# Householder steps of a small eigensolver: divisor from root times size plus square sum, reflector written by VectorE, square sum first on TensorE

## The chip, the core and the metric

The kernel runs on one core of a Trainium2 chip. A core has TensorE (matmuls), VectorE and ScalarE (elementwise work), GpSimd, and DMA queues; each engine runs its own list of instructions in order, and the engines wait for one another by semaphores. The metric is the device time of one execution in microseconds (us), the median of three runs. For this kernel a difference below 0.2% can't be told from none.

## The reference

A two-layer network over x of shape (128, 64, 128), with a normalized adjacency matrix of 64x64. Cut to what matters here:

```python
def _L0_gnn_ref(features, A, W1, b1, W2, b2):
    deg = jnp.sum(A, axis=0) + jnp.sum(A, axis=1) - jnp.diagonal(A)
    d_inv_sqrt = jnp.where(deg > 0, jax.lax.rsqrt(deg), 0.0)
    L = jnp.diag(deg) - A
    L_norm = d_inv_sqrt[:, None] * L * d_inv_sqrt[None, :]
    _, U = jnp.linalg.eigh(L_norm)
    agg = jnp.einsum('mn,bnd->bmd', U.T, features)
    h = jax.nn.relu(agg @ W1 + b1)
    out = h @ W2 + b2
    return jnp.einsum('nm,bmd->bnd', U, out)

x = x + _L0_gnn_ref(_layernorm(x), adj, ...)     # needs all eigenvectors of a 64x64 matrix
x = x + _L0_ffn_ref(_layernorm(x), ...)          # 8 experts, 2 per token
x = x + _L1_gnn_ref(_layernorm(x), adj, ...)     # aggregation, two batch norms
x = x + _L1_ffn_ref(_layernorm(x), ...)          # a shared and 8 routed experts
```

## The kernel before

The program is written by hand, engine by engine: what stands in `tridiagonal_vector` is VectorE's list, `tridiagonal_tensor` TensorE's, `tridiagonal_scalar` ScalarE's. No scheduler moves anything. Before the first layer can start, the eigenvectors of the 64x64 matrix must be there, and everything else of the kernel comes after them. The eigensolver has these stages: preparation (to 13 us), 62 Householder steps that make the matrix tridiagonal (to 193 us), sections that find the eigenvalues, eigenvectors of the tridiagonal matrix, the basis change, and three refinements. The layers follow.

A step k works on the trailing matrix A with t = 63 - k rows and takes the column t as its vector. It has three lists:

- TensorE (L171 to L191) makes six products from the column, broadcast over all partitions: in `ps[0]` its last element alpha, in `ps[1]` its square sum, in `ps[2]` the column's products with A, in `ps[5]` and `ps[3]` rows of A broadcast, in `ps[4]` a product that is only read after the steps. Each counts one up in `hh_pe` (NP = 6 a step).
- VectorE (L133 to L168) makes the sign of alpha (L149), G = sign x root (L151), G(alpha+G) (L152), a guard against zero (L153), the reciprocal (L154), then T = row x G + products (L157), B = T x y - A (L160), a sum over B x VR (L163) and the new A (L167). It counts in `hh_dve` (ND = 9).
- ScalarE (L194 to L222) takes the root (L205), copies the products (L207), writes the reflector v into `VV` (L209), copies the first part of VR (L212), writes y = v x reciprocal into `YY` (L215), VR's tail (L216) and VRT (L218). It counts in `hh_act` (NA = 7). Besides, in the last 54 steps it makes two sums each for the first layer norm (`first_norm_sum`: L1007, L1017), which nothing in the steps needs. A sum is an activation and a read of its accumulator.

The next step's products start when A is written (L183). SBUF tiles of the eigensolver are all named `u` in the profile, PSUM banks `bank`. All tiles of a step begin at partition 0.

Of the kernel before, what the change touches and what calls it, by code (L numbers as in the profile page):

```python
# [8 lines left out]
ALU = mybir.AluOpType  # L9
# [3 lines left out]
N = 64  # L13
P = 128
D = 128
STEPS = N - 2
# [6 lines left out]
ND, NP, NA = 9, 6, 7  # L23
# [109 lines left out]
def tridiagonal_vector(nc, dve, S, E, m, ps):  # L133
# [4 lines left out]
    alpha, row = ps[0][0:N, 0:1], ps[5]  # L138
    for k in range(STEPS):
        t, j = at_step(k)  # L140
        b = k * ND

        def step(n, ins, wait=True):
            ins.then_inc(hd, 1)
            if wait:
                dve.wait_ge(hd, b + n)
        G = SS[:, k:k + 1]
        dve.wait_ge(hp, k * NP + 1)
        step(1, V.tensor_scalar(c[:, 0:1], alpha, 0.0, 2.0, ALU.is_ge, ALU.mult))  # L149
        dve.wait_ge(ha, k * NA + 1)  # L150
        step(2, V.scalar_tensor_tensor(out=G, in0=c[:, 0:1], scalar=-1.0, in1=c[:, 7:8], op0=ALU.add, op1=ALU.mult))  # L151
        step(3, V.scalar_tensor_tensor(out=c[:, 1:2], in0=alpha, scalar=G, in1=G, op0=ALU.add, op1=ALU.mult))  # L152
        step(4, V.tensor_scalar(c[:, 2:3], c[:, 1:2], 1e-36, None, ALU.max))  # L153
        step(5, V.reciprocal(c[:, 6:7], c[:, 2:3]), False)  # L154
        dve.wait_ge(hp, k * NP + 4)
        dve.wait_ge(ha, k * NA + 2)
        step(6, V.scalar_tensor_tensor(out=m["T"][0:t, 0:t], in0=row[0:t, 0:t], scalar=SS[0:t, k:k + 1],  # L157
                                       in1=m["QA"][0:t, 0:t], op0=ALU.mult, op1=ALU.add))
        dve.wait_ge(ha, k * NA + 5)
        step(7, V.scalar_tensor_tensor(out=m["B"][0:t, 0:t], in0=m["T"][0:t, 0:t], scalar=m["YY"][0:t, k:k + 1],  # L160
                                       in1=A[0:t, 0:t], op0=ALU.mult, op1=ALU.subtract))
        dve.wait_ge(ha, k * NA + 6)
        step(8, V.scalar_tensor_tensor(out=m["hjunk"][0:t, 0:t], in0=m["B"][0:t, 0:t], scalar=1.0, in1=m["VR"][0:t, 0:t],  # L163
                                       op0=ALU.mult, op1=ALU.mult, accum_out=c[0:t, 5:6]))
        dve.wait_ge(ha, k * NA + 7)
        dve.wait_ge(hp, k * NP + 6)
        step(9, V.scalar_tensor_tensor(out=A[0:t, 0:t], in0=m["VRT"][0:t, 0:t], scalar=c[0:t, 5:6], in1=m["B"][0:t, 0:t],  # L167
                                       op0=ALU.mult, op1=ALU.subtract))  # L168


def tridiagonal_tensor(nc, pe, S, E, C, m, ps):  # L171
# [5 lines left out]
    for k in range(STEPS):  # L177
# [8 lines left out]
        from_column(ps[0][0:N, 0:1], t, t, unit[0:t, j:j + 1])  # L186
        from_column(ps[1][0:N, 0:1], t, t, A[0:t, t:t + 1])
        from_column(ps[2][0:N, 0:t], t, t, A[0:t, 0:t])
# [5 lines left out]
def tridiagonal_scalar(nc, act, S, E, C, m, ps, t):  # L194
# [3 lines left out]
    A, VR, SS, c = m["AI"][:, N:2 * N], m["VR"], m["SS"], m["c"]  # L198
    unit = C[0:N, C_ID:C_ID + N]
    sums = 0  # L200
    for k in range(STEPS):
        n, j = at_step(k)
        b = k * ND
        act.wait_ge(hp, k * NP + 2)
        F.activation(c[:, 7:8], ps[1][0:N, 0:1], ACT.Sqrt).then_inc(ha, 1)  # L205
        act.wait_ge(hp, k * NP + 3)
        F.copy(m["QA"][0:n, 0:n], ps[2][0:n, 0:n]).then_inc(ha, 1)  # L207
        act.wait_ge(hd, b + 2)
        F.activation(m["VV"][0:n, k:k + 1], unit[0:n, j:j + 1], ACT.Identity, scale=SS[0:n, k:k + 1],  # L209
                     bias=A[0:n, n:n + 1]).then_inc(ha, 1)  # L210
# [3 lines left out]
        act.wait_ge(ha, k * NA + 3)  # L214
        F.activation(m["YY"][0:n, k:k + 1], m["VV"][0:n, k:k + 1], ACT.Copy, scale=c[0:n, 6:7]).then_inc(ha, 1)  # L215
        F.activation(VR[0:n, j:n], ps[3][0:n, j:n], ACT.Identity, bias=SS[0:n, k:k + 1]).then_inc(ha, 1)  # L216
        act.wait_ge(ha, k * NA + 6)
        F.activation(m["VRT"][0:n, 0:n], VR[0:n, 0:n], ACT.Copy, scale=c[0:n, 6:7]).then_inc(ha, 1)  # L218
        if k >= STEPS - EARLY_SUMS // 2:
            first_norm_sum(nc, act, S, E, t, sums)  # L220
            first_norm_sum(nc, act, S, E, t, sums + 1)
            sums += 2  # L222
# [1738 lines left out]
```

## Time and profile before

| | us |
|---|---|
| median of 3 runs | 1445.71 (1445.41 to 1447.09) |
| the profiled execution | 1447.26 |
| its span, first to last instruction | 1445.5 |
| busy over the span: matmul / VectorE / ScalarE / GpSimd | 1094.5 / 934.2 / 650.7 / 605.5 |
| mean granted TensorE clock | 0.936 of full speed |

In the rows below, PE is TensorE's matmuls, PEld its weight loads, DVE VectorE, ACT ScalarE. A group such as `u<-bank 64x1` writes tile u from a PSUM bank, 64 partitions by 1 element. The shares over the whole span say little, since the stages differ: the steps at the head of the kernel are a chain of short instructions on three engines, and the experts at its end keep TensorE full. The page's list of the chain that ended last reaches back only to 1229 us; for the steps one reads the timeline of a single step and the waits.

### The profile page before, as it was taken

How to read it: one execution, taken by the hardware profiler on the slowest of the kernel's cores; microseconds unless marked ns; L12 is line 12 of the kernel's file. 1: busy time of each engine (PE TensorE's matmuls, PEld its weight loads, DVE VectorE, ACT ScalarE, POOL GpSimd, SP SyncE). 2: the span in 40 equal slices, each digit the busy share in tenths (PEclk: the TensorE clock that was granted, in tenths of full speed). 3: DMA queues.
4: the chain of work that ended last, by engine and by line, in shares of the span. 5: the costliest groups of instructions: out<-in, count | busy, mean ns of one | idle time of the engine just before them, and what ended most of it. 6: DMA issues, size and time to landing. Idle time of an engine off the chain costs nothing. (4 is left out here: it accounts for less than half of the span.)

```text
span 1445.5 us, 23166 instructions
## 1 busy us (share of the span) xinstructions
PE 1094.5 (76%) x6172; PEld 887.7 (61%) x6172; DVE 934.2 (65%) x3416; ACT 650.7 (45%) x1813; POOL 605.5 (42%) x591
## 2 busy tenths in 40 slices
PE   3454577514877299999999587779998898899990
PEld 3444465413655288888888443355554797799990
DVE  5555578875788656656667585886743555465673
ACT  3777765600444122222222288547764344344440
POOL 3000000000154777777764530023344677777754
PEclk9999999999998599999999889869999899899995
DMA  9993000000010132222234340000001222222436
GB/s 224 428 428 168 1 2 0 1 0 0 9 38 30 52 81 79 69 87 81 76 110 123 115 159 1 0 14 22 25 30 45 76 87 73 87 84 82 146 104 232
DMA packets 59265, 125.45 MB, mean 87 GB/s; under 512 B 13132, under 2 KB 39636, under 8 KB 57600
## 3 DMA queue, kind: packets, MB, share of 16 engines
q0 software_dynamic: 20000, 73.21, 13.5%
q1 hardware_dynamic: 39136, 50.78, 13.0%
q8 instruction: 50, 0.82, 0.3%
q14 instruction: 79, 0.65, 0.2%
HBM read 50.77 MB, written 74.99 MB: 87 GB/s over the span
## 5 line engine op out<-in xcount | busy, mean ns | idle before, releaser
L891 POOL DMA_INDIRECT rows<-pay,slot x256 | 261.6, 1022 | 483.4 <-issue 432.1
L1224 POOL DMA_INDIRECT planes<-work,goal x284 | 300.1, 1057 | 130.7 <-issue 57.7
L1371 PE MATMUL bank<-pay 128*128 128x128 f32 (+1 forms) x1988 | 276.1, 280 | 0.0
L1371 PEld LDWEIGHTS bank<-pay 128*128 128x128 f32 (+1 forms) x1988 | 263.6, 193 | 10.6 <-DVE pay L1304 0.4
L1331 ACT ACTIVATE pay<-bank,pay 128x256 f32<-128x256 f32 x284 | 125.8, 474 | 167.8 <-PE bank L1362 167.8
L1327 ACT ACTIVATE pay<-bank 128x256 f32<-128x256 f32 (+1 forms) x213 | 81.4, 382 | 246.6 <-PE bank L1360 212.1
L1362 PE MATMUL bank<-pay 128*128 128x256 f32 x568 | 136.9, 385 | 2.2 <-DVE pay L1266 2.2
L1359 PE MATMUL bank<-pay 128*128 128x256 f32 (+1 forms) x426 | 128.9, 384 | 0.6 <-DVE pay L1266 0.6
L181 PE MATMUL bank<-consts,u 63*64 63x1 f32 (+61 forms) x372 | 60.4, 274 | 89.7 <-DVE u L167 88.9
L1360 PE MATMUL bank<-pay 128*128 128x256 f32 (+1 forms) x426 | 128.4, 383 | 0.0
L1304 DVE TENSOR_TENSOR pay<-pay,bank 128x256 f32<-128x256 f32 (+1 forms) x213 | 88.9, 417 | 59.5 <-PE bank L1371 30.7
L1256 DVE COPY pay<-wreg 128x1066 f32 (+1 forms) x142 | 103.6, 730 | 26.8 <-issue 26.8
L1362 PEld LDWEIGHTS bank<-pay 128*128 128x128 f32 x568 | 104.2, 194 | 14.1 <-DVE pay L1256 2.5
L181 PEld LDWEIGHTS bank<-consts,u 63*64 63x64 f32 (+61 forms) x372 | 51.3, 215 | 95.1 <-DVE u L167 94.1
L1360 PEld LDWEIGHTS bank<-pay 128*128 128x128 f32 (+1 forms) x426 | 76.8, 180 | 16.9 <-issue 0.3
L1359 PEld LDWEIGHTS bank<-pay 128*128 128x128 f32 (+1 forms) x426 | 71.5, 181 | 11.2 <-issue 1.1
L1347 PE MATMUL bank<-consts,pay 128*128 128x128 f32 x284 | 55.6, 278 | 27.5 <-DMA pay<-rows 27.5
L1562 PE MATMUL bank<-work,wreg 128*128 128x512 f32 x128 | 65.3, 612 | 5.8 <-ACT work L1617 5.6
L1266 DVE COPY pay<-bank 128x256 f32<-128x256 f32 x142 | 59.4, 418 | 15.3 <-PE bank L1347 15.2
L1278 DVE TENSOR_TENSOR pay<-bank,pay 128x256 f32<-128x256 f32 x71 | 30.1, 424 | 57.9 <-PE bank L1371 57.7
L1555 PE MATMUL bank<-work,wreg 128*128 128x512 f32 x128 | 63.4, 598 | 0.0
L366 PE MATMUL bank<-u,consts 128*128 128x28 f32 (+1 forms) x192 | 54.5, 395 | 7.7 <-DVE u L301 5.6
(399 smaller groups left out, 1988.1 us busy)
## 6 DMA issues: line engine op xcount, KB each, us to landing
rows<-pay POOLq DMA_DIRECT2D x10, 3432.0 KB, 55.7
pay<-rows SPq DMA_DIRECT2D x142, 130.0 KB, 2.2
u<-planes SPq DMA_DIRECT2D x64, 256.0 KB, 3.4
planes<-work,goal POOLq DMA_INDIRECT x284
wreg<-in_w SPq DMA_DIRECT2D x1, 4264.0 KB, 24.8
wreg<-in_w SPq DMA_DIRECT2D x1, 4112.0 KB, 13.4
X<-in_x SPq DMA_DIRECT2D x2, 2048.0 KB, 20.2
rows<-pay,slot POOLq DMA_INDIRECT x256, 2.3
```

Of the source, the lines that this page charges most:

```text
L181: T.matmul(out, A[0:rows, col:col + 1].to_broadcast([rows, N]), rhs, start=True, stop=True).then_inc(hp, 1)
L891: return self.nc.gpsimd.indirect_dma_start(out=xs, out_offset=bass.IndirectOffsetOnAxis(ap=self.t["slot"][:, k, q:q + 1], axis=0), in_=sel ...
L1224: nc.gpsimd.indirect_dma_start(out=planes, out_offset=bass.IndirectOffsetOnAxis(ap=t["goal"][:, j * 2 + h:j * 2 + h + 1], axis=0), in_=t[" ...
L1256: V.tensor_copy(t["wst"][j % 2][:, 0:WB[layer]], W[:, bass.ds(expert * WB[layer], WB[layer])]).then_inc(s("w"), 1)
L1304: V.tensor_tensor(t["hh"][c][0:w, :], t["hs"][c][0:w, :], ps[c][0:w, TS:2 * TS], ALU.mult).then_inc(s("hh"), 1)
L1327: A.activation(t["hs"][c][0:w, :], ps[c][0:w, 0:TS], ACT.Silu).then_inc(s("hs"), 1)
L1331: A.activation(t["hh"][c], ps[c][:, 0:TS], ACT.Gelu, bias=t["wst"][j % 2][:, 2 * CH1 * P + c:2 * CH1 * P + c + 1]).then_inc(s("hh"), 1)
L1359: T.matmul(ps[c][0:n, 0:TS], w[:, a:a + n], x, start=True, stop=True)
L1360: T.matmul(ps[c][0:n, TS:2 * TS], w[:, HID0 + a:HID0 + a + n], x, start=True, stop=True).then_inc(s("up"), 1)
L1362: T.matmul(ps[c][:, 0:TS], w[:, c * P:(c + 1) * P], x, start=True, stop=True).then_inc(s("up"), 1)
L1371: ins = T.matmul(ps[4 + j % 2][:, h * P:(h + 1) * P], t["hh"][c][0:n, h * P:(h + 1) * P], t["wst"][j % 2][0:n, at + c * P:at + (c + 1) * P ...
L1562: T.matmul(ps[4][:, :], t["WS"][:, (CH1 + c) * P:(CH1 + c + 1) * P], t["sh"][c % 2], start=(c == 0), stop=(c == CH1 - 1)).then_inc(S("a1_d ...
```

## The change

- TensorE: the square sum (`ps[1]`) is now the first product, and the second writes two columns of `ps[0]`: alpha and the square sum once more. For this a strided operand takes column j of the identity and column t of A in one product, so the left half of `AI` has to hold the identity; it is copied there once, ahead of the steps.
- VectorE: the divisor is no longer made as G(alpha+G) but as beta = root x size + square sum, with size = sign x alpha, and the guard acts on the square sum. VectorE now writes the reflector v and y itself. 12 instructions a step for 9.
- ScalarE: v and y are gone, 5 counted instructions for 7. VR's tail waits for G, VRT for the reciprocal. One of the two normalization sums moves from the step's end to between the root and the copy of the products.
- The matmuls behind the steps that read `VV` and `YY` wait for VectorE instead of ScalarE.

```diff
 PASSES = len(POINTS)
 REFINE = 3
 BIG = 1e15
-ND, NP, NA = 9, 6, 7
+ND, NP, NA = 12, 6, 5
 LEVELS = 6
 EARLY_SUMS = 108
 SCALE_AT = 9
@@ -130,42 +130,53 @@
     return trailing, trailing - 1
 
 
-def tridiagonal_vector(nc, dve, S, E, m, ps):
+def tridiagonal_vector(nc, dve, S, E, C, m, ps):
 
     V, c, SS = nc.vector, m["c"], m["SS"]
     hd, hp, ha = S("hh_dve"), S("hh_pe"), S("hh_act")
     A = m["AI"][:, N:2 * N]
-    alpha, row = ps[0][0:N, 0:1], ps[5]
+    unit = C[0:N, C_ID:C_ID + N]
+    alpha, square, row = ps[0][0:N, 0:1], ps[0][0:N, 1:2], ps[5]
+    sign, size, guarded, beta, inverse, root = (c[:, i:i + 1] for i in (0, 1, 2, 3, 6, 7))
     for k in range(STEPS):
         t, j = at_step(k)
-        b = k * ND
-
-        def step(n, ins, wait=True):
-            ins.then_inc(hd, 1)
-            if wait:
-                dve.wait_ge(hd, b + n)
-        G = SS[:, k:k + 1]
-        dve.wait_ge(hp, k * NP + 1)
-        step(1, V.tensor_scalar(c[:, 0:1], alpha, 0.0, 2.0, ALU.is_ge, ALU.mult))
+        G, v, y = SS[:, k:k + 1], m["VV"][0:t, k:k + 1], m["YY"][0:t, k:k + 1]
+
+        def done(n):
+            dve.wait_ge(hd, k * ND + n)
+        dve.wait_ge(hp, k * NP + 2)
+        V.tensor_scalar(sign, alpha, 0.0, 2.0, ALU.is_ge, ALU.mult).then_inc(hd, 1)
+        V.tensor_scalar(guarded, square, 1e-36, None, ALU.max).then_inc(hd, 1)
+        done(1)
+        V.scalar_tensor_tensor(out=size, in0=sign, scalar=-1.0, in1=alpha, op0=ALU.add, op1=ALU.mult).then_inc(hd, 1)
+        done(3)
         dve.wait_ge(ha, k * NA + 1)
-        step(2, V.scalar_tensor_tensor(out=G, in0=c[:, 0:1], scalar=-1.0, in1=c[:, 7:8], op0=ALU.add, op1=ALU.mult))
-        step(3, V.scalar_tensor_tensor(out=c[:, 1:2], in0=alpha, scalar=G, in1=G, op0=ALU.add, op1=ALU.mult))
-        step(4, V.tensor_scalar(c[:, 2:3], c[:, 1:2], 1e-36, None, ALU.max))
-        step(5, V.reciprocal(c[:, 6:7], c[:, 2:3]), False)
+        V.scalar_tensor_tensor(out=beta, in0=root, scalar=size, in1=guarded, op0=ALU.mult, op1=ALU.add).then_inc(hd, 1)
+        V.scalar_tensor_tensor(out=G, in0=sign, scalar=-1.0, in1=root, op0=ALU.add, op1=ALU.mult).then_inc(hd, 1)
+        done(4)
+        V.reciprocal(inverse, beta).then_inc(hd, 1)
+        done(5)
+        V.scalar_tensor_tensor(out=v, in0=unit[0:t, j:j + 1], scalar=SS[0:t, k:k + 1], in1=A[0:t, t:t + 1], op0=ALU.mult,
+                               op1=ALU.add).then_inc(hd, 1)
         dve.wait_ge(hp, k * NP + 4)
         dve.wait_ge(ha, k * NA + 2)
-        step(6, V.scalar_tensor_tensor(out=m["T"][0:t, 0:t], in0=row[0:t, 0:t], scalar=SS[0:t, k:k + 1],
-                                       in1=m["QA"][0:t, 0:t], op0=ALU.mult, op1=ALU.add))
+        V.scalar_tensor_tensor(out=m["T"][0:t, 0:t], in0=row[0:t, 0:t], scalar=SS[0:t, k:k + 1],
+                               in1=m["QA"][0:t, 0:t], op0=ALU.mult, op1=ALU.add).then_inc(hd, 1)
+        done(7)
+        V.tensor_tensor(y, v, inverse[0:t, :], ALU.mult).then_inc(hd, 1)
+        done(9)
+        V.scalar_tensor_tensor(out=m["B"][0:t, 0:t], in0=m["T"][0:t, 0:t], scalar=y,
+                               in1=A[0:t, 0:t], op0=ALU.mult, op1=ALU.subtract).then_inc(hd, 1)
+        done(10)
+        dve.wait_ge(ha, k * NA + 4)
+        V.scalar_tensor_tensor(out=m["hjunk"][0:t, 0:t], in0=m["B"][0:t, 0:t], scalar=1.0, in1=m["VR"][0:t, 0:t],
+                               op0=ALU.mult, op1=ALU.mult, accum_out=c[0:t, 5:6]).then_inc(hd, 1)
+        done(11)
         dve.wait_ge(ha, k * NA + 5)
-        step(7, V.scalar_tensor_tensor(out=m["B"][0:t, 0:t], in0=m["T"][0:t, 0:t], scalar=m["YY"][0:t, k:k + 1],
-                                       in1=A[0:t, 0:t], op0=ALU.mult, op1=ALU.subtract))
-        dve.wait_ge(ha, k * NA + 6)
-        step(8, V.scalar_tensor_tensor(out=m["hjunk"][0:t, 0:t], in0=m["B"][0:t, 0:t], scalar=1.0, in1=m["VR"][0:t, 0:t],
-                                       op0=ALU.mult, op1=ALU.mult, accum_out=c[0:t, 5:6]))
-        dve.wait_ge(ha, k * NA + 7)
         dve.wait_ge(hp, k * NP + 6)
-        step(9, V.scalar_tensor_tensor(out=A[0:t, 0:t], in0=m["VRT"][0:t, 0:t], scalar=c[0:t, 5:6], in1=m["B"][0:t, 0:t],
-                                       op0=ALU.mult, op1=ALU.subtract))
+        V.scalar_tensor_tensor(out=A[0:t, 0:t], in0=m["VRT"][0:t, 0:t], scalar=c[0:t, 5:6], in1=m["B"][0:t, 0:t],
+                               op0=ALU.mult, op1=ALU.subtract).then_inc(hd, 1)
+        done(12)
 
 
 def tridiagonal_tensor(nc, pe, S, E, C, m, ps):
@@ -183,8 +194,8 @@
             pe.wait_ge(hd, k * ND)
         else:
             pe.wait_ge(*E.at("lap_flipped"))
-        from_column(ps[0][0:N, 0:1], t, t, unit[0:t, j:j + 1])
         from_column(ps[1][0:N, 0:1], t, t, A[0:t, t:t + 1])
+        from_column(ps[0][0:N, 0:2], t, t, m["AI"][0:t, j:j + N + 2:N + 1])
         from_column(ps[2][0:N, 0:t], t, t, A[0:t, 0:t])
         from_column(ps[5][0:N, 0:t], t, j, unit[0:t, 0:t])
         from_column(ps[3][0:N, 0:t], t, t, unit[0:t, 0:t])
@@ -195,31 +206,28 @@
 
     F = nc.scalar
     hd, hp, ha = S("hh_dve"), S("hh_pe"), S("hh_act")
-    A, VR, SS, c = m["AI"][:, N:2 * N], m["VR"], m["SS"], m["c"]
-    unit = C[0:N, C_ID:C_ID + N]
+    VR, SS, c = m["VR"], m["SS"], m["c"]
     sums = 0
     for k in range(STEPS):
         n, j = at_step(k)
         b = k * ND
-        act.wait_ge(hp, k * NP + 2)
+        act.wait_ge(hp, k * NP + 1)
         F.activation(c[:, 7:8], ps[1][0:N, 0:1], ACT.Sqrt).then_inc(ha, 1)
+        if k >= STEPS - EARLY_SUMS // 2:
+            first_norm_sum(nc, act, S, E, t, sums)
+            sums += 1
         act.wait_ge(hp, k * NP + 3)
         F.copy(m["QA"][0:n, 0:n], ps[2][0:n, 0:n]).then_inc(ha, 1)
-        act.wait_ge(hd, b + 2)
-        F.activation(m["VV"][0:n, k:k + 1], unit[0:n, j:j + 1], ACT.Identity, scale=SS[0:n, k:k + 1],
-                     bias=A[0:n, n:n + 1]).then_inc(ha, 1)
         act.wait_ge(hp, k * NP + 5)
         F.copy(VR[0:n, 0:j], ps[3][0:n, 0:j]).then_inc(ha, 1)
         act.wait_ge(hd, b + 5)
-        act.wait_ge(ha, k * NA + 3)
-        F.activation(m["YY"][0:n, k:k + 1], m["VV"][0:n, k:k + 1], ACT.Copy, scale=c[0:n, 6:7]).then_inc(ha, 1)
         F.activation(VR[0:n, j:n], ps[3][0:n, j:n], ACT.Identity, bias=SS[0:n, k:k + 1]).then_inc(ha, 1)
-        act.wait_ge(ha, k * NA + 6)
+        act.wait_ge(hd, b + 6)
+        act.wait_ge(ha, k * NA + 4)
         F.activation(m["VRT"][0:n, 0:n], VR[0:n, 0:n], ACT.Copy, scale=c[0:n, 6:7]).then_inc(ha, 1)
         if k >= STEPS - EARLY_SUMS // 2:
             first_norm_sum(nc, act, S, E, t, sums)
-            first_norm_sum(nc, act, S, E, t, sums + 1)
-            sums += 2
+            sums += 1
 
 
 def basis_tensor(nc, pe, S, E, C, m, ps):
@@ -227,7 +235,7 @@
 
     T = nc.tensor
     ident, flip = C[0:N, C_ID:C_ID + N], C[0:N, C_FLIP:C_FLIP + N]
-    pe.wait_ge(S("hh_act"), STEPS * NA)
+    pe.wait_ge(S("hh_dve"), STEPS * ND)
     T.matmul(ps[7][0:N, 0:N], m["VV"], m["YY"], start=True, stop=True).then_inc(*E.on("qb_gram"))
     T.matmul(ps[5][0:N, 0:N], m["VV"], flip, start=True, stop=True)
     T.matmul(ps[5][0:N, N:2 * N], m["YY"], flip, start=True, stop=True).then_inc(S("qb_turned"), 1)
@@ -428,11 +436,12 @@
     ch(V.memset(AHB[:, :], 0.0))
     for h in (0, N):
         ch(V.tensor_tensor(AHB[h:h + N, h:h + N], m["Ah"][h:h + N, :], ps[0][h:h + N, N:2 * N], ALU.mult))
+    ch(V.tensor_copy(m["AI"][:, 0:N], ident))
     dve.wait_ge(*E.at("lap_whole"))
     V.tensor_copy(m["AI"][:, N:2 * N], ps[1][0:N, 0:N]).then_inc(*E.on("lap_flipped"))
     dve.wait_ge(*E.at("lap_flipped"))
 
-    tridiagonal_vector(nc, dve, S, E, m, ps)
+    tridiagonal_vector(nc, dve, S, E, C, m, ps)
 
     SS, AI, F = m["SS"], m["AI"], m["F"]
     dve.wait_ge(S("hh_dve"), STEPS * ND)
```

VectorE's list for the first step (63 rows), before. `u1` holds the eigensolver's tiles, `bank0` alpha, `bank5` the broadcast row:

```order
L149 TENSOR_SCALAR u1<-bank0 64x1
L151 SCALAR_TENSOR_TENSOR u1<-u1 64x1
L152 SCALAR_TENSOR_TENSOR u1<-bank0,u1 64x1
L153 TENSOR_SCALAR u1<-u1 64x1
L154 RECIPROCAL u1<-u1 64x1
L157 SCALAR_TENSOR_TENSOR u1<-bank5,u1 63x63
L160 SCALAR_TENSOR_TENSOR u1<-u1 63x63
L163 SCALAR_TENSOR_TENSOR u1<-u1 63x63
L167 SCALAR_TENSOR_TENSOR u1<-u1 63x63
```

The same step after the change:

```order
L441 COPY u1<-bank1 64x64
L148 TENSOR_SCALAR u1<-bank0 64x1
L149 TENSOR_SCALAR u1<-bank0 64x1
L151 SCALAR_TENSOR_TENSOR u1<-u1,bank0 64x1
L154 SCALAR_TENSOR_TENSOR u1<-u1 64x1
L155 SCALAR_TENSOR_TENSOR u1<-u1 64x1
L157 RECIPROCAL u1<-u1 64x1
L159 SCALAR_TENSOR_TENSOR u1<-consts,u1 63x1
L163 SCALAR_TENSOR_TENSOR u1<-bank5,u1 63x63
L166 TENSOR_TENSOR u1<-u1 63x1
L168 SCALAR_TENSOR_TENSOR u1<-u1 63x63
L172 SCALAR_TENSOR_TENSOR u1<-u1 63x63
```

Sign and guard (L148, L149) now stand together, beta (L154) ahead of G (L155), v (L159) ahead of T (L163), and y (L166) between T and B (L168).

ScalarE's list for the step with 52 rows, one with two normalization sums (L1007 before, L1016 after), before:

```order
L205 ACTIVATE u1<-bank1 64x1
L207 COPY u1<-bank2 52x52
L209 ACTIVATE u1<-consts,u1 52x1
L212 COPY u1<-bank3 52x51
L215 ACTIVATE u1<-u1 52x1
L216 ACTIVATE u1<-bank3,u1 52x1
L218 ACTIVATE u1<-u1 52x52
L1007 ACTIVATE u1<-X 128x128 x2
```

The same step after the change:

```order
L215 ACTIVATE u1<-bank1 64x1
L1016 ACTIVATE u1<-X 128x128
L220 COPY u1<-bank2 52x52
L222 COPY u1<-bank3 52x51
L224 ACTIVATE u1<-bank3,u1 52x1
L227 ACTIVATE u1<-u1 52x52
L1016 ACTIVATE u1<-X 128x128
```

v (L209) and y (L215 before) are gone, and the first sum stands behind the root (L215 after).

## Rows read from the trace of the kernel before

**Rows 1.** Busy time by stretch: the steps, then the rest of the eigensolver

```profile
core 0: us, PE busy (x) PEld busy (x) DVE busy (x) ACT busy (x) POOL busy (x), PEclk, DMA share, GB/s
13.40:192.90 179.50, 89.17 (x744) 83.84 (x744) 102.52 (x621) 130.80 (x648) 5.80 (x12) 1.00 0.63 240
192.90:371.00 178.10, 97.94 (x403) 78.74 (x404) 131.65 (x562) 62.76 (x240) 0.00 (x0) 0.99 0.00 1
```

**Rows 2.** Waits from 13 to 193 us: total, times, longest

```profile
DVE u L160 <- ACT u L215: 16.4, 62, 0.3
DVE u L151 <- ACT u L205: 16.4, 62, 0.3
```

**Rows 3.** Timeline of the step with 47 rows: start, duration, instruction, [idle before]

```profile
60.90 0.37 PE L181 MATMUL bank<-consts,u 47*64 47x1 f32 x2 [1.50 <-DVE u L167]
...
61.13 0.64 PE L181 MATMUL bank<-u 47*64 47x1 f32 x4
61.38 0.15 DVE L149 TENSOR_SCALAR u<-bank 64x1 f32<-64x1 f32 x1 [0.54 <-PE bank L181]
...
61.52 0.16 ACT L205 ACTIVATE u<-bank 64x1 f32<-64x1 f32 x1 [0.48 <-PE bank L181]
...
61.79 0.15 DVE L151 SCALAR_TENSOR_TENSOR u<-u 64x1 f32<-64x1 f32 x1 [0.26 <-ACT u L205]
61.80 0.19 ACT L207 COPY u<-bank 47x47 f32<-47x47 f32 x1
...
61.98 0.21 DVE L152 SCALAR_TENSOR_TENSOR u<-bank,u 64x1 f32<-64x1 f32 x1
...
62.22 0.14 DVE L153 TENSOR_SCALAR u<-u 64x1 f32<-64x1 f32 x1
...
62.40 0.15 DVE L154 RECIPROCAL u<-u 64x1 f32<-64x1 f32 x1
62.48 0.26 DVE L157 SCALAR_TENSOR_TENSOR u<-bank,u 47x47 f32<-47x47 f32 x1
62.59 0.29 ACT L215 ACTIVATE u<-u 47x1 f32<-47x1 f32 x1
62.79 0.24 ACT L216 ACTIVATE u<-bank,u 47x1 f32<-47x1 f32 x1
62.99 0.26 DVE L160 SCALAR_TENSOR_TENSOR u<-u 47x47 f32<-47x47 f32 x1 [0.25 <-ACT u L215]
63.06 0.33 ACT L218 ACTIVATE u<-u 47x47 f32<-47x47 f32 x1
63.28 0.20 DVE L163 SCALAR_TENSOR_TENSOR u<-u 47x47 f32<-47x47 f32 x1
...
63.52 0.26 DVE L167 SCALAR_TENSOR_TENSOR u<-u 47x47 f32<-47x47 f32 x1
...
63.84 0.37 PE L181 MATMUL bank<-consts,u 46*64 46x1 f32 x2 [1.50 <-DVE u L167]
```

**Rows 4.** Timeline: VectorE instructions that don't wait for their predecessor

```profile
5.87 0.15 DVE L397 TENSOR_SCALAR u<-u 64x1 f32<-64x1 f32 x1
5.94 0.14 DVE L398 TENSOR_SCALAR u<-u 64x1 f32<-64x1 f32 x1
...
197.03 0.22 DVE L455 TENSOR_SCALAR u<-bank 64x62 f32<-64x62 f32 x1
197.16 0.14 DVE L456 COPY u<-bank 64x1 f32<-64x1 f32 x1
```

**Rows 5.** All instructions of L157: duration in ns, shortest, median, longest

```profile
L157 DVE SCALAR_TENSOR_TENSOR u<-bank,u x62: 207/241/275, 15.0 to 191.6; 63x63 f32<-63x63 f32 x1, 62x62 f32<-62x62 f32 x1, 61x61 f32<-61x61 f32 x1, 60x60 f32<-60x60 f32 x1
```

**Rows 6.** Timeline of ScalarE: two normalization sums in a late step

```profile
189.58 0.38 ACT L1017 ACTIVATE u<-X,u 128x128 f32<-128x128 f32 x1
...
189.97 0.38 ACT L1017 ACTIVATE u<-X,u 128x128 f32<-128x128 f32 x1
```

**Rows 7.** Timeline of VectorE just ahead of the first step

```profile
12.62 0.47 DVE L430 TENSOR_TENSOR AHB<-u,bank 64x64 f32<-64x64 f32 x2
13.13 0.22 DVE L432 COPY u<-bank 64x64 f32<-64x64 f32 x1
```

## The prediction

> **What bounds the kernel now.** I read first the busy time by stretch. From 13.40 to 192.90 us the kernel does only the 62 Householder steps: 179.5 us with TensorE's matmuls busy for 89, VectorE for 103 and ScalarE for 131 [rows 1]. No engine is full, so this stretch is a chain of waits. 179.5/62 is 2.90 us a step. The stretch behind it, to 371 us, has no DMA traffic to speak of (1 GB/s) and VectorE busy for 132 of 178 us [rows 1]: the rest of the eigensolver is a VectorE chain that starts from the last step. What a step loses or gains therefore moves everything behind it.
>
> Next, who waits for whom in that stretch. Besides the waits at the step's start for TensorE, VectorE waits twice for ScalarE in every step: 62 times at L151 for the square root and 62 times at L160 for y from L215, 16.4 us each, so 0.26 us a time [rows 2].
>
> Then one step in order of time, that with 47 rows (it starts at 60.90, the next at 63.84: 2.94 us) [rows 3]. I count from its first matmul (t = 0). VectorE reads alpha's sign at 0.48 (L149), ScalarE takes the root at 0.62 (L205), and the chain runs L151 0.89, L152 1.08, L153 1.32, L154 1.50, L215 on ScalarE 1.69, L160 2.09, L163 2.38, L167 2.62, next matmul 2.94. T (L157, 1.58) and the work of L207, L216 and L218 lie beside it. Each of these starts is the end of the one before plus a handover, which the rows give: 0.04 within VectorE (61.79+0.15 to 61.98), 0.04 VectorE to ScalarE (62.55 to 62.59), 0.11 ScalarE to VectorE (62.88 to 62.99), 0.06 VectorE to TensorE.
>
> **What an instruction costs if nothing waits for it.** The change puts three VectorE instructions more into a step (12 for 9) and three ScalarE instructions less of its own chain (5 for 7, and one normalization sum moved), so it matters how long an instruction keeps the engine's queue. Rows show it: L154 starts at 62.40 and lasts 0.15, yet L157 starts at 62.48 [rows 3]; L397 to L398 is 0.07 at 0.15 of duration; L455, which reads a bank, gives way after 0.13 of 0.22 [rows 4]. So a successor that does not wait starts about 0.08 before the duration ends; a dependent one 0.04 after. I use both.
>
> **The new step, part by part** (t from its first matmul).
> The matmul order: the square sum is now first, alpha and the square sum together second. The spacing of two products is 0.23 (60.90 to 61.13) [rows 3]. The root's input comes one product earlier, so the root starts at 0.62-0.22 = 0.40 and is there for VectorE at 0.40+0.16+0.11 = 0.67. VectorE's first instruction waits for the second product: 0.48+0.22 = 0.70, a loss of 0.22 at the start that the removed wait of 0.26 about pays for.
> Sign 0.70; "guarded" in its shadow at 0.77. Size needs the sign: 0.70+0.15+0.04 = 0.89. It has a constant scalar, as L151 (0.15); with a pointer scalar the form takes 0.21 (L152) [rows 3]. Beta (root times size plus guarded, pointer scalar) 0.89+0.19 = 1.08; the root is ready since 0.67, so ScalarE leaves this part of the chain. G may follow beta after 0.21-0.08 = 0.13: 1.21. The reciprocal needs beta: 1.33. The reflector v needs G: 1.21+0.19 = 1.40, which is also when the reciprocal gives way. v has a pointer scalar (0.21) and ends at 1.61. T takes its shadow at 1.53 and keeps the queue for its duration less 0.08; it lasts 0.207 to 0.275, median 0.241 [rows 5], so until 1.66 to 1.73, 1.69 at the median. y needs v (1.65) and the queue: 1.69. It lasts 0.15, and B starts at 1.69+0.19 = 1.88 (1.85 to 1.92).
> Before, B (L160) started at 2.09 [rows 3]. Behind B nothing changes: the same three instructions with the same handovers. Gain 0.21 a step; I take off 0.01 for beta, which now has a second, already satisfied wait (L167 with three waits comes 0.02 later behind its predecessor than the others), and get 0.20. 62 x 0.20 = 12.4 us.
>
> What must stay hidden. T needs the copy of the products, at 0.90 (L207), done at 1.09 and visible at 1.20, against T at 1.53. The tail of VR needs G: 1.36+0.04 = 1.40. Ahead of it in ScalarE's queue stands the copy of VR's first part, whose product is two spacings (0.43) behind that which L207 waits for: 1.33, so the tail starts at some 1.43 and ends at 1.67, 1.78 for VectorE, against the junk product at 1.88+0.29 = 2.17. VRT follows the tail by 0.27 and lasts 0.33: 2.03, visible at 2.14, against the last instruction at 1.88+0.53 = 2.41. Slack 0.27; if it went, each excess would count 62 times. The sum now between root and product copy, in 54 of the steps, keeps ScalarE for 0.39 in its longer form (189.58 to 189.97) [rows 6]: from 0.48 to 0.87, before the copy's 0.90. The sum that remains at the end runs into the next step's idle time of ScalarE.
> One copy of the identity (64x64) is added ahead of the steps, before L432, which does not wait for TensorE in the trace (it stands right behind L430) [rows 7]. So it is on the path, once: about L432's own 0.22 us.
> The final wait for the reflectors costs nothing: the last of them are now written before the last A.
>
> **Sum.** 12.4-0.2 = 12.2 us off. The profiled execution took 1447.26 us with a span of 1445.5; it becomes 1435.1, its span 1433.3. The median of the runs, 1445.71, lies 1.55 below that execution, so the forecast is 1445.71-12.2 = 1433.5 us.
>
> **Where the Trainium skill says otherwise.** The bank read at L149 lasts 0.151 us, the same kind of instruction on SBUF 0.15 (L397) [rows 3, 4]. The Trainium skill, page "VectorE: DVE Perf Modes", section on the TRN2 errata, has a fixed 120 cycles for a PSUM source against 58 for SBUF at 0.96 GHz, an estimate of 0.065 us more. By that rule "size", which reads alpha from a bank, would add 0.065 to each step and the sum would be 8.2 us; by the trace it adds nothing.
>
> **Rivals.**
> (a) The queue costs less than I reckon, or the second product reaches VectorE earlier. If T did not delay y (B at 1.84) and the sign started at 0.66 instead of 0.70, half way to ScalarE's 0.62: gain 0.29, 18.0-0.2 = 17.8 us, 1427.9. For it: ScalarE sees the second product at 0.62. Against: VectorE's own 0.48 for the first product is a steady row.
> (b) The queue costs more: T, reading a bank and SBUF with a pointer, holds y for its whole duration (y at 1.53+0.24+0.04 = 1.81, B at 2.00), or a bank read that lasts 0.21 delays size by 0.06, or both. Gain 0.03 to 0.15; at 0.09 it is 5.6-0.2 = 5.4 us, 1440.3. No row has a short instruction right behind one of T's form, so this is open.
> (c) The other sign: VectorE does not overlap in this mix, each instruction starts only when its predecessor has ended. Place: the nine instructions from sign to y. Price: 0.151+0.151+0.151+0.21+0.151+0.155+0.21+0.241+0.15 = 1.57 and nine handovers of 0.03 (a dependent pair takes 0.04): B at 0.70+1.57+0.27 = 2.54, 0.45 later than now, +28 us, 1474. It decides from the point where the added queue time exceeds 0.20 a step. Against: the shadow of L154 over L157 in this very loop. The Trainium skill, same page, section "The DRAIN you can't avoid", says that after every operation the next one does not start until the pipe is empty; that would be this case. The trace speaks against it in rows 3 and 4.
> (d) No gain to see: ScalarE becomes late behind its own queue (VRT past 2.41 by some 0.2 or more), or a stretch of lower TensorE clock behind the eigensolver falls differently and takes the gain. Result 1443 to 1448. Against: 0.27 of slack, and the clock was 1.00 and 0.99 in the two stretches up to 371 us [rows 1].
> (e) The change does not do what it says: VectorE still waits for the root or for ScalarE's y. The first has 0.41 of slack (0.67 against 1.08), the second no longer exists. I give it nothing of its own.
>
> **Chances.** Forecast 0.64 (its own range 1430 to 1437), (a) 0.10, (b) 0.18, (d) 0.04, (c) 0.04. The range for 8 in 10 takes the forecast and the nearer part of (a) and (b): 1428 to 1440. A difference of over 0.2% (2.9 us) can be told from none for this kernel; (b) lies below 1442.8 in nearly all of its span. Faster 0.92, the same 0.04, slower 0.04.
>
> **What the profile after would show.** A step of about 2.74 us at 47 rows and a stretch of steps of about 167 us; no wait of VectorE for ScalarE at all; sign at 0.70, beta at 1.08, v at 1.40, B at 1.88 behind the first matmul; the root at 0.40 and the product copy still at 0.90 behind a sum. Wrong would be: y more than 0.2 behind T (b), G more than 0.2 behind beta (c), a wait of VectorE for ScalarE at the junk product or the last instruction (d). The stretches behind the steps should keep their lengths; if one does not, the sum is wrong though each step is right.

## The result, and the profile after

| | before | after |
|---|---|---|
| median of 4 runs each, us | 1446.33 | 1432.59 |
| ratio, 95% interval | | 0.9907 (0.9895 to 0.9919) |
| span of the profiled execution, us | 1445.5 | 1430.5 |
| the 62 steps, first matmul to the diagonal's read | 179.5 | 166.0 |

The change gained 13.7 us; 12.2 were forecast (1433.5 us), and 1432.6 lies in the range. The two spans differ by more, 15.0, because the profiled execution before (1447.26 us) was longer than its kernel's median. Busy time by stretch, the steps and the rest of the eigensolver, as [rows 1]:

```profile
core 0: us, PE busy (x) PEld busy (x) DVE busy (x) ACT busy (x) POOL busy (x), PEclk, DMA share, GB/s
13.60:179.60 166.00, 89.17 (x744) 83.82 (x744) 109.46 (x806) 96.08 (x525) 5.80 (x12) 1.00 0.68 260
179.60:357.70 178.10, 97.12 (x412) 77.95 (x413) 132.31 (x566) 62.90 (x240) 0.00 (x0) 1.00 0.00 1
```

The second stretch has kept its length. VectorE does 7 us more in the steps, ScalarE 35 less. Waits from 13 to 181 us (total, times, longest): those of [rows 2] are gone, and what VectorE still waits for in every step is TensorE at its start.

```profile
PE bank L192 <- DVE u L177: 75.7, 61, 1.6
ACT u L215 <- PE bank L192: 49.8, 62, 6.1
DVE u L148 <- PE bank L192: 46.7, 62, 1.1
```

The step with 47 rows, as [rows 3] (start, duration, instruction):

```profile
58.33 0.87 PE L192 MATMUL bank<-u 47*64 47x1 f32 x6 [1.37 <-DVE u L177]
58.73 0.16 ACT L215 ACTIVATE u<-bank 64x1 f32<-64x1 f32 x1 [0.81 <-PE bank L192]
...
59.02 0.15 DVE L148 TENSOR_SCALAR u<-bank 64x1 f32<-64x1 f32 x1 [0.75 <-PE bank L192]
59.10 0.14 DVE L149 TENSOR_SCALAR u<-bank 64x1 f32<-64x1 f32 x1
59.21 0.15 DVE L151 SCALAR_TENSOR_TENSOR u<-u,bank 64x1 f32<-64x1 f32 x1
...
59.39 0.21 DVE L154 SCALAR_TENSOR_TENSOR u<-u 64x1 f32<-64x1 f32 x1
...
59.52 0.14 DVE L155 SCALAR_TENSOR_TENSOR u<-u 64x1 f32<-64x1 f32 x1
59.63 0.15 DVE L157 RECIPROCAL u<-u 64x1 f32<-64x1 f32 x1
...
59.71 0.20 DVE L159 SCALAR_TENSOR_TENSOR u<-consts,u 47x1 f32<-47x1 f32 x1
...
59.84 0.25 DVE L163 SCALAR_TENSOR_TENSOR u<-bank,u 47x47 f32<-47x47 f32 x1
60.02 0.14 DVE L166 TENSOR_TENSOR u<-u 47x1 f32<-47x1 f32 x1
...
60.19 0.26 DVE L168 SCALAR_TENSOR_TENSOR u<-u 47x47 f32<-47x47 f32 x1
...
61.04 0.87 PE L192 MATMUL bank<-u 46*64 46x1 f32 x6 [1.28 <-DVE u L177]
```

Counted from the step's first matmul: sign 0.69 (forecast 0.70), size 0.88 (0.89), beta 1.06 (1.08), G 1.19 (1.21), v 1.38 (1.40), T 1.51 (1.53), y 1.69 (1.69), B 1.86 (1.88), next step 2.71 (2.74). The copy of the identity takes 0.22 ahead of the steps (13.10 to 13.32), as reckoned.

### The profile page after: what moved, and what is told of

Read it like the earlier page. It is cut to its first block and busy times, and to the rows that moved or that the text cites. A ratio compares the mean times of both kernels' runs of the same rounds, so it can differ in the third digit from the quotient of the medians.

```text
span 1430.5 us, 23168 instructions
## 1 busy us (share of the span) xinstructions
PE 1092.2 (76%) x6172; PEld 885.5 (62%) x6172; DVE 941.3 (66%) x3603; ACT 615.7 (43%) x1689; POOL 605.2 (42%) x591
## 5 line engine op out<-in xcount | busy, mean ns | idle before, releaser
L1380 PEld LDWEIGHTS bank<-pay 128*128 128x128 f32 (+1 forms) x1988 | 263.4, 193 | 10.7 <-DVE pay L1313 0.7
L192 PE MATMUL bank<-u 63*64 63x1 f32 (+61 forms) x496 | 73.7, 255 | 76.8 <-DVE u L177 75.7
L192 PEld LDWEIGHTS bank<-u 63*64 63x64 f32 (+61 forms) x496 | 64.4, 217 | 82.2 <-DVE u L177 80.9
## 6 DMA issues: line engine op xcount, KB each, us to landing
wreg<-in_w SPq DMA_DIRECT2D x1, 4112.0 KB, 13.3
```

Source lines behind the costliest of these rows:

```text
L192: T.matmul(out, A[0:rows, col:col + 1].to_broadcast([rows, N]), rhs, start=True, stop=True).then_inc(hp, 1)
L1380: ins = T.matmul(ps[4 + j % 2][:, h * P:(h + 1) * P], t["hh"][c][0:n, h * P:(h + 1) * P], t["wst"][j % 2][0:n, at + c * P:at + (c + 1) * P ...
```

## The experiments

Twelve kernels ran. The kernel before took 1445.92 us beside the first four, 1445.53 beside the next four and 1445.56 beside the last four; each ratio goes by its own. "At n rows" is a step; times in a step count from its first matmul.

For small differences the end of the steps is the better measure than the total. Far behind them lies a stretch that no edit touches, from the first layer's last product (L1070 in the changed kernel) to the last mixing product (L1491). In the fourteen profiled executions it took 428.4 to 428.7 us in four and 430.4 to 433.9 in the others, so up to some 3 us of a difference between two kernels need not come from the steps. The steps end where the next stage first reads the diagonal: at 192.9 us before and at 179.6 in the changed kernel.

**Alpha first.** The first two products swapped back:

```diff
-        from_column(ps[1][0:N, 0:1], t, t, A[0:t, t:t + 1])
         from_column(ps[0][0:N, 0:2], t, t, m["AI"][0:t, j:j + N + 2:N + 1])
+        from_column(ps[1][0:N, 0:1], t, t, A[0:t, t:t + 1])
```

(VectorE waits for the first product, ScalarE for the second.)

> The changed kernel with TensorE's first two products swapped back: alpha with the square sum first, the root's square sum second. My theory (starts follow from durations, 0.04 us for a dependent instruction, duration less 0.08 for one that does not wait): sign 0.48, size 0.67, root visible at 0.62+0.27 = 0.89, so beta at 0.89 instead of 1.06 and B some 0.17 earlier; T at 1.34 needs the product copy, which the sum ahead of it delays to about the same time. Step with 47 rows 2.54 us against 2.71, in all 62 x 0.17 = 10.5 us below the changed kernel: 1422. That the square sum comes first would then be the one harmful part of the change. Rival theory: the root is what the chain waits for, and putting the square sum first is part of the gain; then this kernel is slower than the changed one by up to 62 x 0.2 = 12 us, and VectorE waits at beta for ScalarE from 0.9 to 1.1.

Measured 1423.34 us, 0.9840 (0.9824 to 0.9857) of before, 9.3 below the changed kernel; the steps end at 170.1 us, 9.5 earlier. The timeline at 43 rows (its first matmul at 66.30):

```profile
66.78 0.15 DVE L148 TENSOR_SCALAR u<-bank 64x1 f32<-64x1 f32 x1 [0.54 <-PE bank L192]
...
66.92 0.17 ACT L215 ACTIVATE u<-bank 64x1 f32<-64x1 f32 x1 [0.78 <-PE bank L192]
...
67.20 0.21 DVE L154 SCALAR_TENSOR_TENSOR u<-u 64x1 f32<-64x1 f32 x1
...
68.00 0.25 DVE L168 SCALAR_TENSOR_TENSOR u<-u 43x43 f32<-43x43 f32 x1
```

Beta starts at 0.90, B at 1.70, 0.16 earlier. "Square sum first" feeds the root, which had 0.4 us of slack, and holds up alpha, which had none: that part of the change costs 9 us. The rival falls.

**Reflector only.** The old divisor and the old order of products, one product column, no copy of the identity; v and y stay on VectorE (part of the edit against the changed kernel):

```diff
+        V.scalar_tensor_tensor(out=size, in0=alpha, scalar=G, in1=G, op0=ALU.add, op1=ALU.mult).then_inc(hd, 1)
         V.scalar_tensor_tensor(out=v, in0=unit[0:t, j:j + 1], scalar=SS[0:t, k:k + 1], in1=A[0:t, t:t + 1], op0=ALU.mult,
                                op1=ALU.add).then_inc(hd, 1)
+        done(3)
+        V.tensor_scalar(guarded, size, 1e-36, None, ALU.max).then_inc(hd, 1)
+        done(5)
+        V.reciprocal(inverse, guarded).then_inc(hd, 1)
...
```

> One part alone: v and y on VectorE; divisor G(alpha+G) with its guard, and the order of the products, as before the change. Theory: sign 0.48, G 0.89, u 1.08, v behind it at 1.21, guard 1.33, reciprocal 1.51, T 1.59, y 1.75, B 1.93 against 2.09 before: 0.16 a step, 10 us, 1436.4. So most of the gain of the whole change (13.7 us) comes from this part. Rival: the new divisor, which takes one dependent instruction off the chain, brings most of it, and this kernel stays at 1441 to 1446.

Measured 1434.92 us, 0.9923 (0.9906 to 0.9939): 11.0 us less than before, against 13.7 for the whole change. By the steps alone it is less: they end 8.7 us earlier (at 184.2), against 13.3. B at 1.95 (43 rows) to 1.89 (3 rows). Alpha first has the same products' order and the new divisor besides, and its steps end 14.1 us before those of this kernel (11.6 by the medians). So the new divisor is worth much more than this run and the changed kernel suggest, once alpha comes first.

**Reflector on ScalarE.** The other part alone:

```diff
+        act.wait_ge(hd, b + 5)
+        F.activation(m["VV"][0:n, k:k + 1], unit[0:n, j:j + 1], ACT.Identity, scale=SS[0:n, k:k + 1],
+                     bias=A[0:n, n:n + 1]).then_inc(ha, 1)
...
+        F.activation(m["YY"][0:n, k:k + 1], m["VV"][0:n, k:k + 1], ACT.Copy, scale=c[0:n, 6:7]).then_inc(ha, 1)
```

> The other part alone: new divisor, square sum first, but v and y back on ScalarE (10 VectorE instructions, 7 of ScalarE; one normalization sum still behind the root). Theory: G is there only at 1.34 (0.89+0.15 = 1.04 before the change), v on ScalarE at 1.38 lasts 0.39, y at 1.81 lasts 0.29, visible 2.21, so B at 2.21: 0.12 a step later than before and 0.35 later than the changed kernel. 1446.3+7.6 = 1454, slower than both. Rival: y's wait was only 0.26 a step and the shorter divisor pays for it; then 1436 to 1446.

Measured 1456.64 us, 1.0074 (1.0058 to 1.0091), slower than before by 10.7; the steps end 12.0 us later. At 43 rows (first matmul at 76.98):

```profile
78.18 0.14 DVE L155 SCALAR_TENSOR_TENSOR u<-u 64x1 f32<-64x1 f32 x1
...
78.36 0.39 ACT L220 ACTIVATE u<-consts,u 43x1 f32<-43x1 f32 x1 [0.29 <-DVE u L155]
...
78.84 0.29 ACT L226 ACTIVATE u<-u 43x1 f32<-43x1 f32 x1
...
79.24 0.26 DVE L165 SCALAR_TENSOR_TENSOR u<-u 43x43 f32<-43x43 f32 x1 [0.53 <-ACT u L226]
```

G at 1.20 instead of 0.89 sends v and y off late; VectorE now waits 0.53 at B. The two parts do not add up: 11.0 gained by the one, 10.7 lost by the other, 13.7 gained together.

**Sums last.** Both normalization sums at the step's end again (the call between root and product copy moved behind VRT):

```diff
-        if k >= STEPS - EARLY_SUMS // 2:
-            first_norm_sum(nc, act, S, E, t, sums)
-            sums += 1
...
-            sums += 1
+            first_norm_sum(nc, act, S, E, t, sums + 1)
+            sums += 2
```

> The changed kernel with both normalization sums back at the step's end. Theory: they end in ScalarE's idle time (last sum free at 1.72+0.21+0.78 = 2.71, the next root 0.41 behind a step of 2.5 to 2.7), and the one behind the root never delayed the product copy enough to count (T at 1.51, copy visible at 1.15): same time as the changed kernel, 1432.6 within 1.5. Rival: the moved sum is needed for the gain, because two sums at the end push the next root; then up to 54 x 0.1 = 5 us slower.

Measured 1432.11 us, 0.9907 (0.9890 to 0.9923): the move is worth nothing here; the steps end within 0.2 us of the changed kernel's.

**Alpha first, sums last.** Both edits.

> Alpha first as in the run of that name, and both normalization sums back at the step's end. There the product copy started at 1.08 in the late steps behind the longer sum, at 0.84 without it, and T at 1.35 just had it. Theory: T starts at 1.35 by G (1.04), v (1.23) and the queue, not by the copy, so nothing is gained: 1423.3 within 1.5. Rival: T waited for the copy (visible at 1.08+0.15+0.11 = 1.34) and moves to 1.32: 22 steps x 0.03 = 0.7 us, hardly to be told; a gain of over 2 us would mean that ScalarE's queue was on the chain in more places.

Measured 1422.72 us, 0.9833 (0.9812 to 0.9853). T starts at 1.35 as with alpha first alone (43 rows). No gain that can be told.

**G ahead.** The kernel above with VectorE's order changed, and with it the counts that ScalarE waits for:

```diff
+        dve.wait_ge(ha, k * NA + 1)
+        V.scalar_tensor_tensor(out=G, in0=sign, scalar=-1.0, in1=root, op0=ALU.add, op1=ALU.mult).then_inc(hd, 1)
         done(3)
-        dve.wait_ge(ha, k * NA + 1)
         V.scalar_tensor_tensor(out=beta, in0=root, scalar=size, in1=guarded, op0=ALU.mult, op1=ALU.add).then_inc(hd, 1)
-        V.scalar_tensor_tensor(out=G, in0=sign, scalar=-1.0, in1=root, op0=ALU.add, op1=ALU.mult).then_inc(hd, 1)
         done(4)
-        V.reciprocal(inverse, beta).then_inc(hd, 1)
-        done(5)
         V.scalar_tensor_tensor(out=v, ...)
+        done(5)
+        V.reciprocal(inverse, beta).then_inc(hd, 1)
```

> Alpha first, sums last, and on VectorE the order sign, guard, size, G, beta, v, reciprocal, T, y, B: G and v no longer stand behind beta. Theory: the root is visible at 0.89, G 0.90, beta in its shadow 0.98, v 1.11, reciprocal 1.23, T 1.31, y (T's 0.25 less 0.08 behind it) 1.48, B 1.65 at 47 rows, against 1.70 with beta first. 0.05 a step: 3 us below the 1423.3 of alpha first, 1420.3. Rival: the reciprocal, now behind v, sets y (1.23+0.155+0.04 = 1.43, so not) or ScalarE's VRT becomes late (visible 2.10+0.11 against the last instruction at 2.18): then no gain, 1423.

Measured 1416.49 us, 0.9789 (0.9767 to 0.9810), 6.2 below the kernel with both edits where 3 were expected. B starts at 1.57 at 43 rows where 1.65 was expected, since G starts at 0.82 and not at 0.90: 0.04 behind the root's end (0.62+0.16). Before and in the kernel above it was 0.11. There VectorE's instruction behind the root had two waits, here it has one. The timeline at 43 rows (first matmul at 64.89):

```profile
66.46 0.25 DVE L168 SCALAR_TENSOR_TENSOR u<-u 43x43 f32<-43x43 f32 x1
66.66 0.33 ACT L224 ACTIVATE u<-u 43x43 f32<-43x43 f32 x1
...
66.88 0.07 DVE L172 DVE_READ_ACCUMULATOR u<-u 43x1 f32 x1
67.08 0.25 DVE L177 SCALAR_TENSOR_TENSOR u<-u 43x43 f32<-43x43 f32 x1
```

But the 0.08 does not explain the 3 us of surplus. B is 0.13 earlier than in the kernel above, the last instruction (L177) only 0.04: it starts 0.13 behind the accumulator's read where 0.04 was the rule, and 0.09 behind VRT (L224), which has become the limit. The steps end 3.8 us earlier, near the 3 expected; the other 2.4 us lie behind them.

**G ahead, 16 commands.** A command is an entry of VectorE's list: an instruction, a wait that stands in front of one, or the read of an accumulator. A long step takes 0.08 to 0.36 us more than its neighbours. VectorE's wait for its own last instruction goes:

```diff
-        done(12)
```

> The kernel with G ahead, without VectorE's wait for its own last instruction at the end of each step (TensorE waits for it anyway, and VectorE for TensorE). The changed kernel shows steps that are 0.1 to 0.36 us too long every seventh to eighth step, and each time one instruction further on in the step; the kernel before shows none. Theory: VectorE's instructions are fetched in blocks of 128 (8.2 KB, if each wait beyond the first counts as one), and with 18 of them a step the border creeps through the step. This kernel has 16 a step, so long steps come every eighth step and always at the same instruction, or are not to be seen at all. Time within 1.5 us of the kernel with G ahead (its own stalls make some 1.7 us). Rival: the long steps come from memory traffic; then their places do not change with the count.

Measured 1414.72 us, 0.9781 (0.9760 to 0.9802). The timeline at 43 rows (first matmul at 64.58):

```profile
64.99 0.15 DVE L148 TENSOR_SCALAR u<-bank 64x1 f32<-64x1 f32 x1 [0.46 <-PE bank L191]
...
65.20 0.16 ACT L214 ACTIVATE u<-bank 64x1 f32<-64x1 f32 x1 [0.44 <-PE bank L191]
...
65.39 0.15 DVE L153 SCALAR_TENSOR_TENSOR u<-u 64x1 f32<-64x1 f32 x1
...
66.34 0.33 ACT L223 ACTIVATE u<-u 43x43 f32<-43x43 f32 x1
66.44 0.20 DVE L172 SCALAR_TENSOR_TENSOR u<-u 43x43 f32<-43x43 f32 x1
66.56 0.07 DVE L172 DVE_READ_ACCUMULATOR u<-u 43x1 f32 x1
...
66.76 0.25 DVE L177 SCALAR_TENSOR_TENSOR u<-u 43x43 f32<-43x43 f32 x1
```

Sign at 0.41, where it was 0.48 with a second wait; G hangs on the root, so this gives nothing. The steps end 1.0 us earlier than with G ahead (by the medians 1.8, where at most 1.5 was expected): the regular long steps (0.1 to 0.35 us, 1.2 us in all there) are gone, but for one at step 47 (counted from 0). That one is ScalarE's: VRT starts 0.27 us late, and it does so in all five kernels made from the changed one that have both sums at the step's end, and in no other. L177 waits for VRT (L223) as above.

**Before, shifted.** Three no-operations of VectorE ahead of the first step.

```diff
+    for _ in range(3):
+        V.nop()
```

> The kernel before with three VectorE no-operations ahead of the first step and nothing else. It has 9 instructions and 7 further waits a step, 16, so the border of a block of 128 falls on the same place of every eighth step. Theory: if that place was a covered one, moving it by three shows long steps (0.1 to 0.36 us) every eighth step, up to 8 x 0.3 = 2.4 us: 1446 to 1448.3. Rival: no long step at all and the same time, because long steps need a denser queue than the kernel before has.

Measured 1445.63 us, 0.9998 (0.9988 to 1.0007), no long step. But the run does not test the theory. The trace has no record of the three no-operations, and the border did not move: the 8192-byte packet of queue q14 ("instruction" on the page) which follows step 41's L153 by 0.72 us before (135.44 us, 122.0 behind the first matmul) follows it by 0.72 here too (135.58, again 122.0). What it shows is that the kernel before has such a border about L153 and no long step there.

**Before, waits in the other order.** At L149, L151 and L160:

```diff
         dve.wait_ge(ha, k * NA + 1)
+        dve.wait_ge(hd, b + 1)
...
         dve.wait_ge(ha, k * NA + 5)
+        dve.wait_ge(hd, b + 6)
```

(The own waits stood ahead of those for ScalarE; likewise at L149 for TensorE.)

> The kernel before, with the same instructions, where VectorE's wait for another engine and its wait for its own last result are written the other way round at L149, L151 and L160. In the built program one wait rides on the instruction and the other becomes a command of its own in front. Till now VectorE's own counter, long satisfied, rode on it and the other engine's, which comes last, stood in front. The runs show 0.07 more behind such a wait: sign 0.48 behind the step's start against 0.41 without the own wait, root to G 0.27 against 0.20. Theory: 3 waits x 0.07 x 62 = 13 us, 1433, as much as the whole change gained, with nothing computed otherwise (TensorE's, ScalarE's lists unchanged). ScalarE's v and y may come to be the limit, then less: 8 to 13 us. Rival: the 0.07 comes from the number of waits, not from which one comes last; then the time stays at 1445.7.

Measured 1438.24 us, 0.9955 (0.9938 to 0.9972): 7.3 us gained by the order of waits alone. At 43 rows (first matmul at 70.16):

```profile
70.56 0.15 DVE L151 TENSOR_SCALAR u<-bank 64x1 f32<-64x1 f32 x1 [0.46 <-PE bank L185]
...
70.78 0.16 ACT L209 ACTIVATE u<-bank 64x1 f32<-64x1 f32 x1 [0.44 <-PE bank L185]
...
70.97 0.15 DVE L154 SCALAR_TENSOR_TENSOR u<-u 64x1 f32<-64x1 f32 x1 [0.26 <-ACT u L209]
...
71.77 0.29 ACT L219 ACTIVATE u<-u 43x1 f32<-43x1 f32 x1
...
72.10 0.26 DVE L164 SCALAR_TENSOR_TENSOR u<-u 43x43 f32<-43x43 f32 x1 [0.18 <-ACT u L219]
```

Each handover is 0.07 shorter (root to G 0.19, was 0.27; y to B 0.33, was 0.40), but the sign's is covered by the root and VRT holds back the last instruction (2.51, with VRT's end at 2.42): 0.10 a step reach the end, not 0.21; the steps end 6.2 us earlier. The mechanism stands, my sum missed two covers.

**After, without the own wait.** The line `done(12)` removed from the changed kernel.

> The changed kernel without VectorE's wait for its own last instruction at each step's end, nothing else. Theory: sign at 0.62 instead of 0.69, and since the whole chain hangs on it in this kernel, 0.07 a step, 4.3 us, 1428.3. Commands a step 17 instead of 18, so long steps remain, about every 7.5 steps. Rival: the own wait was free, as it was satisfied long before: 1432.6.

Measured 1424.62 us, 0.9862 (0.9845 to 0.9878), 8.0 below the changed kernel, where 4.3 were expected. At 43 rows (first matmul at 67.46):

```profile
68.08 0.15 DVE L148 TENSOR_SCALAR u<-bank 64x1 f32<-64x1 f32 x1 [0.68 <-PE bank L191]
...
69.25 0.25 DVE L168 SCALAR_TENSOR_TENSOR u<-u 43x43 f32<-43x43 f32 x1
```

Sign 0.62, B 1.79, each 0.07 earlier. The steps end at 174.4 instead of 179.6 us: 5.2, of which 4.3 are the 0.07 and most of the rest fewer long steps. The other 3 us come far behind, from the stretch named above, which the edit does not touch: it takes 428.7 us here, 432.3 in the changed kernel, 432.2 before. In the expert stage, 100 us of this kernel (first row) and of the changed one (second), at the same distance from the first layer:

```profile
534.30:634.30 100.00, 98.24 (x604) 87.24 (x603) 63.69 (x164) 26.80 (x70) 78.05 (x73) 1.00 0.28 81
```

```profile
539.40:639.40 100.00, 96.25 (x582) 85.51 (x582) 61.18 (x157) 25.83 (x68) 78.04 (x73) 0.98 0.28 79
```

The granted clock is 1.00 against 0.98, and TensorE gets 22 matmuls more done in the same time. That is not all of it: the tuned kernel below has 0.98 in this window and 428.7 us all the same. Why an execution falls on one side or the other stays open; one execution of each kernel was profiled.

**Before, 17 commands.** The line `dve.wait_ge(ha, k * NA + 1)` once more, ahead of the reciprocal.

> The kernel before with one more wait, satisfied long before, in front of the reciprocal: 17 commands a step in VectorE's list (accumulator read counted) instead of 16. All kernels with 17 or 18 showed steps that are up to 0.36 us too long every seventh or eighth step, the three with 16 showed none. Theory: with 17 long steps appear in the kernel before too, 1 to 2 us in all, 1446 to 1448. Rival: they come with VectorE's dense queue and not with the count, then there are none here.

Measured 1444.65 us, 0.9992 (0.9982 to 1.0001). Long steps at 8, 23, 31 and 38 (0.15 to 0.36 us), the steps end at 194.0 instead of 192.9: as the theory says. The total does not show it (1446 to 1448 was expected), and its interval reaches to no difference. In the profiled execution the stretch behind was a short one (428.5 us), which fits, but that this holds for all its runs is not shown.

**Tuned.** On top of the 16 commands:

```diff
-        done(11)
         dve.wait_ge(ha, k * NA + 5)
-        dve.wait_ge(hp, k * NP + 6)
+        done(11)
...
+        act.wait_ge(hp, k * NP + 6)
```

> The kernel with G ahead and 16 commands, where the last instruction of a step takes its wait for ScalarE's VRT on itself, its own counter in front, and the wait for TensorE's sixth product goes to ScalarE ahead of VRT. In the kernel with G ahead VRT has become the limit: it starts at 1.76 and lasts 0.32, and the last instruction starts 0.11 later at 2.18, 0.13 behind the accumulator read instead of 0.04. Theory: now the later of VRT plus 0.04 (2.12) and the sum plus 0.04 plus 0.07 (2.16): 0.03 a step, 1.5 to 2 us, 1413. Rival: VRT, now with two waits of its own, starts 0.07 later and eats it: 1414 to 1417.

Measured 1414.20 us, 0.9786 (0.9770 to 0.9802). The steps end at 164.2 instead of 165.5 us, 0.02 a step; the medians can't tell the two apart. The last instruction starts 0.10 behind the accumulator's read (0.13 with 16 commands), its own counter's wait now being the late one in front, and VRT is not later for its third wait (1.76, was 1.77). It is the fastest of all: 18.4 us below the changed kernel and 31.4 below before.

## Why the prediction was right

- **The steps set the end.** Right. The steps became 13.5 us shorter; with 0.2 us for the copy, the first product of the first layer came 13.4 us earlier (333.7 for 347.1). The rest, up to 13.7 by the medians, is within what the stretches behind them scatter.
- **How long an instruction keeps the queue** (duration less 0.08, else 0.04 behind). Right, and the reason why ten of eleven starts at 47 rows came out within 0.02 (the reciprocal at 1.30 for 1.33). y's 1.69 is exact by luck: T came 0.02 early and held the queue for 0.18, not 0.16. It also settles rival (b): T does not hold y for its whole 0.25. Rival (c), VectorE without overlap, is refuted by the same rows, and size, which reads a bank, lasted 0.148, not 0.065 more. Rival (c) quotes half a section: the Trainium skill, page "VectorE: DVE Perf Modes", section "The DRAIN you can't avoid", adds that a next instruction that is not held starts earlier, and with that the trace agrees (guard 0.08 behind sign, which lasts 0.15).
- **B at 1.88, gain 0.20.** A little low: B came at 1.88 (63 rows) to 1.82 (3 rows). I used T's median; v lasted 0.20 and y 0.14 for my 0.21 and 0.15, and the 0.01 for beta's second wait was not there. I had it from a misread row: between L163 and L167 stands an accumulator's read, and L167 starts the usual 0.04 behind that one's end. Without the long steps the gain is (13.5+1.6)/62 = 0.24 a step.
- **Not foreseen: long steps,** 1.6 us in all, for instance at 55 rows, where size starts at 36.94 and beta, which follows after 0.18 elsewhere, at 37.39:

```profile
36.94 0.15 DVE L151 SCALAR_TENSOR_TENSOR u<-u,bank 64x1 f32<-64x1 f32 x1
37.39 0.21 DVE L154 SCALAR_TENSOR_TENSOR u<-u 64x1 f32<-64x1 f32 x1 [0.30 <-ACT u L220]
```

  They took back most of what the low estimate missed, so the sum was nearer than its terms: that is luck.
- **"A loss of 0.22 at the start that the removed wait of 0.26 about pays for".** True as a sum, and I stopped there: I did not ask what the order of the products gives by itself. Alpha first shows that the loss was needless, 9.3 us.
- **The handover of 0.11 from ScalarE** I read from the rows as the price of the engine. It is 0.04 and a second wait of 0.07: G ahead and the wait order show it at the root and at y, the missing own wait shows the same 0.07 at the wait for TensorE. The sum did not suffer, since it kept or removed such pairs whole. It also names the cause of part of the gain: both waits that the change took away were of the dear kind.
- **What must stay hidden.** All of it did in the changed kernel, but VRT's slack was 0.20 and not 0.27. VRT has two waits now and starts 0.09 behind the tail's end, where before, with one, it was 0.03 (62.79+0.24 to 63.06); so it ends at 2.10, and the last instruction at 2.40 could start 0.09 behind that. In the kernels with G ahead the slack is used up.

## What to carry to other kernels

In a chain of short instructions, write down for each its inputs' ready times and lay them out by two numbers from the trace: how soon a dependent one starts, and how long an independent one blocks the queue. Then try each order on paper: an input with slack must not go ahead of one without, and what can't be split (a new divisor and the engine of the reflector) must be judged together. Of two waits in front of an instruction, let that which comes last ride on the instruction (here: write it first), and drop waits that another engine's wait implies.

## What the runs showed of the hardware

- A second wait of an instruction is a command of its own. If the late one stands in front, VectorE's instruction starts 0.07 us later (sign at 0.48 against 0.41, 0.69 against 0.62; root to G 0.27 against 0.19), ScalarE's VRT 0.06 (0.09 behind the tail against 0.03); if it is the early one, nothing (L151 to L154: 0.04 behind the end, with two waits).
- Nine kernels with 17 or 18 VectorE commands a step have regular long steps. Counted over VectorE's list from the first step's first command as 0, the late command of the changed kernel is number 21, 149, 277, 405, 533, 661, 789, 917 and 1045, each 128 behind the last, and it is the same within one in the other eight. Not all of them lengthen the step. From step 43 on, an 8192-byte packet of q14 ("instruction" on the page) follows each late command of the changed kernel by 0.64 to 0.66 us. So the long steps stand at the borders of blocks of 128 commands.
- Five kernels with 16 commands a step have none. The kernel before crosses such borders too (the packets follow command number 661, 789 and 917 by 0.71 to 0.72 us) without a late start. Why is not explained.
- Not tried is a single product for alpha and the square sum, which alpha first would lead to. The Trainium skill, page "PSUM — Partial Sum Buffer", section "PSUM bank collisions raise a hardware error", says that two engines may not access one bank in the same 32-partition quadrant at once, reads included; no run here shows it. By that rule ScalarE's root can't take its square sum from the bank that VectorE reads alpha from at the same time.
